# A decoder layer with a mixture of experts on one core: four weight slots freed by halves, and the shared expert computed feature-major

## What is computed

```
logits = x @ Wg
probs = jax.nn.softmax(logits, axis=-1)
vals, idx = jax.lax.top_k(probs, TOP_K)
weights = vals / (jnp.sum(vals, axis=-1, keepdims=True) + EPS)
hpre = jnp.einsum('th,ehf->tef', x, W1) + b1
act = jax.nn.silu(hpre)
y = jnp.einsum('tef,efh->teh', act, W2) + b2
out = jnp.einsum('te,teh->th', cw, y)
shared = jax.nn.silu(x @ Ws1 + bs1) @ Ws2 + bs2
out = out + SHARED_SCALE * shared
```

## Time and profile before

| | |
|---|---|
| median of 3 runs | 1330.91 us (1330.57 to 1333.17) |
| the profiled execution | 1336.1 us, span 1334.3 us |
| PE busy | 1060.5 us (79% of the span) |
| DVE busy | 922.7 us (69%) |
| POOL busy | 781.7 us (59%) |
| ACT busy | 541.6 us (41%) |
| moved by DMA | 131.72 MB, 99 GB/s over the span |

### The profile page before, as it was taken

How to read it: one execution, slowest core, us unless ns; L and a number is a source line. 1 busy time by engine, 2 the same in 40 slices (tenths; PEclk the granted TensorE clock), 3 DMA queues, 4 the chain that set the end, 5 groups by cost and what they waited for, 6 DMA issues and landing times.

```text
span 1334.3 us, 15024 instructions
## 1 busy us (share of the span) xinstructions
PE 1060.5 (79%) x4952; PEld 732.0 (55%) x4952; DVE 922.7 (69%) x1066; ACT 541.6 (41%) x1186; POOL 781.7 (59%) x469
## 2 busy tenths in 40 slices
PE   7696676668677677766767699999999899888885
PEld 5343333324333243333433368899999766777775
DVE  5968998998989989898998955556656530111110
ACT  2686443443434444344443421344544431222221
POOL 4255998998989989899898933634321004011111
PEclk9876888998988889898997999799999989999998
DMA  4001344444444434344454502310000007387884
GB/s 158 0 13 37 100 111 93 105 108 91 107 93 106 109 93 104 90 114 101 91 110 88 107 15 76 119 55 12 12 0 0 0 1 265 117 251 231 273 257 132
DMA packets 95707, 131.72 MB, mean 99 GB/s; under 512 B 12153, under 2 KB 89098, under 8 KB 95626
## 3 DMA queue, kind: packets, MB, share of 16 engines
q1 hardware_dynamic: 91738, 126.59, 35.8%
q0 software_dynamic: 3904, 4.33, 1.7%
HBM read 122.48 MB, written 9.23 MB: 99 GB/s over the span
## 4 chain that ended last, share of the span: by engine, by line
PE 33%; issue 26%; DVE 25%; DMA 6%; POOL 4%; SPq 2%; ACT 1%; DVEq 0%; POOLq 0%; ACTq 0%
DVE states L1490 13%; DVE states L1502 10%; PE ps L990 7%; DMA w_tile<-in_w 6%; PE ps L1165 5%; PE ps L1335 4%; PE ps L983 3%; PE ps L1348 3%; PE ps L1149 3%; PE ps L1311 2%; PE ps L1057 2%; PE ps L1048 2%; PE ps L1294 2%; POOL dt L583 1%; POOL dtu L587 1%
## 5 line engine op out<-in xcount | busy, mean ns | idle before, releaser
L606 POOL TENSOR_TENSOR states<-states,c_row 128x800 f32<-128x800 f32 x255 | 474.6, 1884 | 59.5 <-DVE states L1502 59.2
L1502 DVE TENSOR_TENSOR_SCAN states<-ps,states 128x800 f32<-128x800 f32 x256 | 459.3, 1813 | 0.0
L839 ACT ACTIVATE ps<-dt,neg_a 128x396 f32<-128x396 f32 x512 | 283.5, 585 | 362.7 <-DVE states L1502 362.7
L1057 PE MATMUL ps<-states,ident 128*128 128x400 f32 x1024 | 416.6, 542 | 1.9 <-POOL states L606 1.9
L1057 PEld LDWEIGHTS ps<-states,ident 128*128 128x128 f32 x1024 | 210.7, 209 | 142.2 <-issue 53.3
L1490 DVE TENSOR_TENSOR states<-dtu,ps 128x800 f32<-128x800 f32 x192 | 185.1, 964 | 32.1 <-PE ps L1039 29.3
L1039 PE MATMUL ps<-b_parts,row_sel 96*128 96x400 bf16 x192 | 68.7, 359 | 161.6 <-DVE states L1490 156.8
L1039 PEld LDWEIGHTS ps<-b_parts,row_sel 96*128 96x128 bf16 x192 | 19.0, 99 | 237.5 <-DVE states L1490 220.5
L727 POOL DMA_INDIRECT sums<-y_tile,x_tile x20 | 30.9, 1546 | 175.0 <-DVE y_tile L1762 136.4
L597 POOL TENSOR_TENSOR states<-dtu,b_row 128x800 f32<-128x800 f32 x64 | 121.2, 1893 | 0.0
L888 ACT ACTIVATE probs<-ps,shift 100x361 f32<-100x361 f32 x128 | 70.8, 559 | 102.6 <-DVE shift L1581 102.6
(11 more groups left out here) (216 smaller groups left out, 1403.8 us busy)
## 6 DMA issues: line engine op xcount, KB each, us to landing
c_row<-rows SPq DMA_DIRECT2D x256, 200.0 KB, 3.2
w_tile<-in_w SPq DMA_DIRECT2D x40, 1024.0 KB, 7.9
b_row<-rows SPq DMA_DIRECT2D x64, 200.0 KB, 4.2
ctx<-in_ctxT SPq DMA_DIRECT2D x8, 361.0 KB, 4.4
rows_by_slot<-blank_rows SPq DMA_DIRECT2D x1, 2660.0 KB, 11.6
x_tile<-rows_by_slot SPq DMA_DIRECT2D x20, 133.0 KB, 8.0
win<-in_winT SPq DMA_DIRECT2D x2, 1024.0 KB, 9.2
w_shared<-in_w SPq DMA_DIRECT2D x2, 1024.0 KB, 6.1
```

The costliest lines, as they stand in the source:

```text
L606: nc.gpsimd.tensor_tensor(st, st, c_row[i % C_SLOTS][:].unsqueeze(1).broadcast_to([P, CP, TQ]), ALU.mult).then_inc(product_ready, 1)
L839: nc.scalar.activation(seqs(decay[i % DECAYS][:, j * TQ:(j + 1) * TQ])[:, :, 1:], seqs(dt_sb[d][:, c, chunk(q)])[:, :, 1:], ACT.Exp, scale ...
L1057: mm = nc.tensor.matmul(ps[:, j, 0:TQ], ident[:], states[i % RING][:, j * TQ:(j + 1) * TQ], start=False, stop=(i % N == N - 1), skip_group ...
L1502: nc.vector.tensor_tensor_scan(st, decay[i % DECAYS], st, 0.0, ALU.mult, ALU.add).then_inc(scan_done, 1)
```

## The change

It has three parts. The weights get four slots, and a slot is given back in halves: W1 and the bias when ACT has taken the silus of the tile in it, W2 when PE has finished it (`load_first`, `load_second`, with semaphores w1_in and w2_in, for which `into_tile` and `out_of_tile` now wait). All five row slots are filled at first, and on SP's queue the rows of tile k+1 follow the weights of tile k. The shared expert's second product becomes feature-major (128 features x 400 tokens, summed in PSUM banks 4 to 7) and runs two units behind the first; its result is copied to `shared_sum` by DVE and ACT, turned to token-major by PE (`turn_shared`) and then added to x (`set_sums`). And `turned` uses the transpose where it multiplied by `ident`. The sum in DRAM and its chain of adds stay as they are.

```
-W_SLOTS, X_SLOTS = 3, 5
+W_SLOTS, X_SLOTS = 4, 5
...
-ROW_BANKS = (2, 6)
+ROW_BANKS = (2, 3)
+SHARED_LAG = 2
...
             def load_weights(k):
-                r = k % W_SLOTS
-                if k >= W_SLOTS:
-
-                    sp.wait_ge(tile_done, k - W_SLOTS + 1)
+                r, turn = k % W_SLOTS, k - W_SLOTS + 1
                 e = sp.value_load(expert_of[0:1, k:k + 1], min_val=0, max_val=E - 1)
-                load_expert(w_tile[r], e, w_in[r])
+                if turn > 0:
+
+                    sp.wait_ge(tile_silu, FT * turn)
+                load_first(w_tile[r], e, w1_in[r])
+                if turn > 0:
+
+                    sp.wait_ge(tile_done, turn)
+                load_second(w_tile[r], e, w2_in[r])
...
             sp.wait_ge(scattered, 16 * PICKS * B)
-            for k in range(W_SLOTS):
+            for k in range(X_SLOTS):
                 load_rows(k)
...
             for k in range(W_SLOTS, TILES):
-                load_rows(k)
                 load_weights(k)
+                if k + 1 < TILES:
+                    load_rows(k + 1)
...
+            for q in range(Q):
+                act.wait_ge(shared_done, q + 1)
+                nc.scalar.activation(shared_sum[:, 1, chunk(q)], ps[:, 4 + 2 * q + 1, 0:TQ], ACT.Copy
+                                     ).then_inc(shared_copied[1], 1)
...
                 for b in range(BQ):
-                    mm = nc.tensor.matmul(bank(key)[:, b * L:(b + 1) * L], src(q * BQ + b), how, start=True, stop=True)
+                    to = bank(key)[:, b * L:(b + 1) * L]
+                    if how is order[0]:
+                        mm = nc.tensor.transpose(to, src(q * BQ + b), how)
+                    else:
+                        mm = nc.tensor.matmul(to, src(q * BQ + b), how, start=True, stop=True)
...
+            def shared_second(u):
+                q, ft = divmod(u, FT)
+                pe.wait_ge(silu_done, u + 1)
+                for m in range(KD):
+                    nc.tensor.matmul(ps[:, 4 + 2 * q + m, 0:TQ],
+                                     w_shared[:, W2_AT + ft * D + m * P:W2_AT + ft * D + (m + 1) * P],
+                                     hidden[:, ft, chunk(q)], start=(ft == 0), stop=False)
+
+            pe.wait_ge(shared_in, W1_LOADED + 16)
+            for u in range(UNITS):
+                shared_first(u)
                 if u == LOGITS_AT:
                     logits()
+                    pe.wait_ge(route_consts, ROUTE_CONSTS)
                 if u == RANKS_AT:
                     ranks()
                 if u == ROWS_AT:
                     weight_rows()
-
+                if u >= SHARED_LAG:
+                    shared_second(u - SHARED_LAG)
+            for u in range(UNITS - SHARED_LAG, UNITS):
+                shared_second(u)
             pe.wait_ge(cwT_ready, Q)
-            pe.wait_ge(silu_done, UNITS)
-            for b in range(B):
-                to = ps[0:L, 4 + b // 2, b % 2 * D:(b % 2 + 1) * D]
-                nc.tensor.matmul(to, cwT[:, b * L:(b + 1) * L], b2_sb[:], start=True, stop=False)
-                for ft in range(FT):
-                    mm = nc.tensor.matmul(to, hidden[:, ft, b * L:(b + 1) * L],
-                                          w_shared[:, W2_AT + ft * D:W2_AT + (ft + 1) * D],
-                                          start=False, stop=(ft == FT - 1))
-                if b % 2:
-                    mm.then_inc(shared_done, 1)
+            for q in range(Q):
+                for m in range(KD):
+                    mm = nc.tensor.matmul(ps[:, 4 + 2 * q + m, 0:TQ], b2_sb[:, tile(m)], cwT[:, chunk(q)],
+                                          start=False, stop=True)
+                mm.then_inc(shared_done, 1)
+
+            def turn_shared(h):
+                if h % 2 == 0:
+                    for by in shared_copied:
+                        pe.wait_ge(by, h // 2 + 1)
+                for j in range(2):
+                    b = 2 * h + j
+                    for m in range(KD):
+                        mm = nc.tensor.transpose(ps[0:L, 4 + h, j * D + m * P:j * D + (m + 1) * P],
+                                                 shared_sum[:, m, b * L:(b + 1) * L], ident[:])
+                mm.then_inc(shared_turned, 1)
...
             turn_tile(0)
             turn_tile(1)
+            for h in range(2):
+                turn_shared(h)
             into_tile(0)
+            for h in range(2, B // 2):
+                turn_shared(h)
...
+            def set_sums(h):
+                dve.wait_ge(shared_turned, h + 1)
                 nc.vector.tensor_tensor(out_tok[:, pair(h), :].rearrange("l b d -> l (b d)"),
                                         x_tok[:, pair(h), :].rearrange("l b d -> l (b d)"), ps[0:L, 4 + h, :], ALU.add
                                         ).then_inc(out_ready, 1)
+
+            for q in range(Q):
+                dve.wait_ge(shared_done, q + 1)
+                nc.vector.tensor_copy(shared_sum[:, 0, chunk(q)], ps[:, 4 + 2 * q, 0:TQ]).then_inc(shared_copied[0], 1)
...
             take_tile(0)
             take_tile(1)
+            for h in range(B // 2):
+                set_sums(h)
```

More of the change, by code:

```diff
@@ L87 @@
 MIXW, MOEW = 16 * 11, 16 * 2
-LOADED = 16 * 3
+W1_LOADED = 16 * 2
 V_TAP, V_CONVB, V_BDT, V_D, V_ALOG = 0, TAPS, TAPS + 1, TAPS + 2, TAPS + 3
@@ L268, in decoder_layer @@
         weight = [sb(f"weight{r}", [P, 1], scope=moe) for r in range(2)]
+        shared_sum = sb("shared_sum", [P, KD, T], scope=moe)
         hidden = sb("hidden", [P, FT, T], scope=moe)
@@ L308, in decoder_layer @@
         scattered = sem("scattered")
-        w_in = [sem(f"w_in{r}") for r in range(W_SLOTS)]
+        w1_in = [sem(f"w1_in{r}") for r in range(W_SLOTS)]
+        w2_in = [sem(f"w2_in{r}") for r in range(W_SLOTS)]
         rows_in = [sem(f"rows_in{r}") for r in range(X_SLOTS)]
         shared_done = sem("shared_done")
+        shared_copied = [sem("shared_copied_by_dve"), sem("shared_copied_by_act")]
+        shared_turned = sem("shared_turned")
         sums_set = sem("sums_set")
@@ L487, in load_expert, with load_second @@
                 sp.dma_start(to[:, B1_AT:WP], b1[at].rearrange("e p f -> p (e f)")).then_inc(signal, 16)
+            def load_second(to, e, signal):
                 sp.dma_start(to[:, W2_AT:B1_AT].rearrange("p (f d) -> p f d", f=FT),
-                             w2[at].rearrange("e (f p) d -> p (e f) d", p=P)).then_inc(signal, 16)
+                             w2[bass.ds(e, 1)].rearrange("e (f p) d -> p (e f) d", p=P)).then_inc(signal, 16)
             job_copied(sp, ("fuse", B // 2 - 1))
-            load_expert(w_shared, E, shared_in)
+            load_first(w_shared, E, shared_in)
+            load_second(w_shared, E, shared_in)
             sp.dma_start(wg_sb[:], wg.rearrange("(k p) e -> p k e", p=P)).then_inc(moew_in, 16)
@@ L690, in _ @@
                                     allow_small_or_imprecise_dtypes=True))
-            pool.wait_ge(shared_in, LOADED)
+            pool.wait_ge(shared_in, W1_LOADED + 16)
             shared_out = w_shared[:, W2_AT:B1_AT]
@@ L1278, in weight_rows @@
                 pe.wait_ge(cw_ready, 1)
+                pe.wait_ge(slots_ready, 1)
                 for b in range(B):
@@ L1282, in weight_rows, with shared_first @@
                 mm.then_inc(cwT_done, 1)
-            pe.wait_ge(shared_in, LOADED)
-            for u in range(UNITS):
+            def shared_first(u):
                 q, ft = divmod(u, FT)
@@ L1344, in out_of_tile @@
                     pe.wait_ge(tile_weighed, k - 1)
+                pe.wait_ge(w2_in[k % W_SLOTS], 16 * (k // W_SLOTS + 1))
                 w = w_tile[k % W_SLOTS]
@@ L1738, in _ @@
             experts()
-            for h in range(B // 2):
-                dve.wait_ge(shared_done, h + 1)
+            def set_sums(h):
+                dve.wait_ge(shared_turned, h + 1)
                 nc.vector.tensor_tensor(out_tok[:, pair(h), :].rearrange("l b d -> l (b d)"),
```

6 lines of the change are left out of this document (3 added, 3 removed).

## The result

The changed kernel takes 1295.89 us (median of 4 runs, 1293.87 to 1298.24) against 1332.04 us of the kernel before (4 runs, 1330.57 to 1337.64): ratio 0.9722, 95% interval 0.9685 to 0.9758. That is 36 us less, and 2 us under the low end of the predicted range. The profiled execution took 1293.94 us, with a span of 1292.2.

The account below looks back on a forecast made before the run. It took the last 190 us, routed tiles waiting for weights with adds close behind, as the bound. Tile stage 20.8 us plus head 0 off the 1334.3 us span gave 1313.5, or 1310 from the median; range 1298 to 1327.

Parts of the forecast that it names:

- The sum's first term: Tile stage: sixteen add steps at 8.4 us and three at 4.55, 148.1 us instead of 168.85, a gain of 20.8.
- three floors under the 8.89: Tile stage, 8.89 us per add step: adds 8.2 to 8.65, transfers 7.7, PE 7.25, none moved by the change.
- PE then follows the adds: Tile stage after the change: weights' slack of about 5 us is used up and the adds set the pace, 8.4 us.
- The sign that was to tell the two apart: Profile after, tile stage: adds released nearly all by the landing before; released by y_tile throughout would mean PE or transfers bound.
- Halving the slot gains nothing more: Weight loads: rows waiting for tile_added hold weights until near 10 us after tile_done of k-4, later than either half is free.
- The whole head gives nothing: Before the tile stage: PE's saved work becomes a wait for rows, into_tile(1) stays at 1148.0; bounds gain 5.0, loss 2.
- the fourth load ahead of the rows: Head: four tiles of weights instead of three load ahead of the rows, 5.4 us more.
- nothing of it arrives: Kernel start: transposes free PE 3.4 us earlier, but DVE's and POOL's work adds up, so no gain.
- E: Tile stage: PE floor of 7.25 us a step, end near 1292; given no chance of its own.
- B: Tile stage: adds land in 6.9 us or less and transfers of 7.7 us bound, 1298.9 us; chance 0.15.
- C: Tile stage: adds slow to 10.5 us a step beside never-pausing transfers, kernel slower at 1343.8 us; chance 0.12.
- D: Head: rows arrive 5 us later than forecast and adds step at 9.28 us, 1329 us, no change; chance 0.06.

## Why the prediction was right or wrong

**Which step failed.** The sum's first term: "Sixteen steps have weights beside them ... 16 x 8.4 + 3 x 4.55 = 148.1 us". Its form held, its size did not: the sixteen steps took 7.47 each and the last three 14.59, 134.1 in all. Those 14.0 us account for the miss (1310.1 - 14.0 = 1296.1, measured 1295.9). That the rest of the sum then fits to 0.2 us is chance: the stage with the old loading took 165.2 to 168.9 us in four profiles, and the head with the old shared expert 91.8 to 96.3 in five. The figure of 8.4 came from five steps of before and from the median landing there, 7.4 us. "The three floors under the 8.89 are therefore 8.2 to 8.65 (adds), 7.7 (transfers) and 7.25 (PE), and the change moves none of them" was the error: measured apart they are 7.45, at most 6.5, and 7.25. The first had been read while the weights set the rhythm, the second from a busy share. What made the few landings of before slower than those of the changed kernel stays open.

**Bound.** Right that the weights paced the kernel before (two sums changed nothing there, a fourth slot gave some 29 us). "PE then follows the adds" was wrong by a hair: TensorE sets the end, the adds cost 1.0 us. The sign that was to tell the two apart did not: landings ended 16 of 19 steps, as forecast for adds that pace, although TensorE paced.

**Halves.** "Halving the slot gains nothing more" was right with four slots, and its reason too: SP waited for landings in 15 waits, 75.4 us. The prediction did not see that three slots, with halves and the new order, would do as well.

**Head.** "The whole head gives nothing" was right against the one profile of before, in part by luck: 91.8 us there; 92.8, and 91.8 again, in the changed kernel. But of five profiles with the old shared expert only two have 91.8; the others have 94.4, 95.1 and 96.3, with a granted clock of 0.92 to 0.94 from the first unit to the first turn where the two have 0.99. Against those the head gains some 2 to 4 us. The mechanism was right (TensorE's saved work stands as a wait for x_tile, forecast at some 8 us, 6.64 measured where no stall hides it; slot_idx forecast near 1104, 1098.34 in the profile that began the experts 8.7 us early, 1104.24 and 1104.44 in two later ones). The forecast that slot_idx comes 6.8 us later behind the first unit holds at a like clock: 32.4 us in the changed kernel profiled again (clock 0.88) against 25.8 to 26.3 with the old shared expert (0.83 and 0.84). The 22.99 of the profile of before had a clock of 0.97, so that pair of profiles shows 9.7. One part was off: the fourth load ahead of the rows costs 3.5 us (heads of 88.2 and 88.4 with three slots, 91.8 with four), not 5.4.

**Transposes.** Of the start "nothing of it arrives" was wrong for the mixers, which begin 2.1 us sooner, and nearly right for the attention, where 0.4 us are left. The 1.2 us ahead of the attention did not show for the same reason, the lower clock behind the transposes. The second half of xn3T was put at 0.9; both halves together gave 2.1.

**Rivals.** E, TensorE's floor at 7.25 us and an end near 1292, was given no chance because a transfer floor of 7.7 stood above it; it was the nearest in mechanism. B (1298.9), 3.0 us off, was nearer in number, by chance: it had the adds landing in 6.9 us or less, which happened (6.5), but with transfers as the bound, which they aren't. C and D did not occur. On the Trainium skill's rule (TensorE: Matmul & The Clock Gate, Part 4: PE-mode transpose) that transposes don't count as busy: the granted clock stood at 0.53 from 1065 to 1071 us and 0.75 from 1071 to 1077 in the changed kernel, behind transposes, and at 0.50 for both in the kernel before, behind plain products, whose units also began later, so that row doesn't decide it. The product with `wfuse_sb` agrees with the rule: 0.50 to 0.75 where half of the products ahead of it are transposes, 1.00 where none is. But the transposes there also take half the time and leave TensorE idle for 1.5 us, and no run separates the two. The time by the rule, 0.9 us longer, did not show in the one pair profiled on one chip: the 2.1 us reach slot_idx there, which comes 41.8 us behind the last product with wo in the changed kernel and 44.0 without the transposes.

## What to carry to other kernels

A floor read while another wait sets the rhythm is too high: find it by taking the bound's own work away (half a product left out) before trusting it. Take a transfer floor from bytes over the highest rate that any stretch of the trace shows, not from the busy share. When one resource lacks a few microseconds of lead, the cheapest single cure (here one more slot) can give nearly all of the gain, and what is issued ahead of the first use then costs time at the head. Work saved on an engine can be paid back in its clock: look at the granted clock of the stretch behind it.

## What the runs showed of the hardware

- Most of the spread between runs of one kernel goes with the granted clock. Of the kernel before, one execution had 1322.88 us at a mean clock of 0.925, another 1338.79 at 0.909; over the 19 executions measured with these two, time and clock correlate at -0.95. Two single profiles can so differ by 7 us in a part that the change doesn't touch.
- Where half of the products of `turned` are transposes, with a pause of 1.5 us behind the last of them, the granted clock was 0.50 to 0.75 over the 6 us around the start of the product with `wfuse_sb`, in fourteen of fourteen profiles; where all are plain products it was 1.00, in six of six. With the transposes alone that product took 15.63 us instead of 13.98.
- The DMA share exceeded 1 (1.09 at 362 GB/s, 0.92 at 278 over the changed kernel's stage), so it is no measure of room left.
- ScalarE stood 3.4 to 6.9 us at a time for something that the profile calls remote while weights moved: with the new shared expert in six of eleven profiles with four tiles' weights ahead of the x rows, in neither of two with three tiles', and in one of two with two tiles' (3.65 us; there the rows came early enough that TensorE stood 2.63 us behind it, and the head was 86.5 instead of 83.8 us); with the old shared expert in none of five. What brings it about in one execution and not in another is open.
